# Moving the split of the cross values' weights onto GpSimd, with the context ahead of its folds

## The reference, cut to what matters

```python
ln_out = _ln(hidden_states, ln_w, ln_b)
q  = _fp8_linear_pertensor(ln_out, wq, wq_scale, q_in_scale)    # likewise k, v, qx
kvx = jnp.einsum('bsi,oi->bso', cond, w_kv_x)
kx, vx = jnp.split(kvx, 2, axis=-1)
...
xout = _gqa(qx, kx, vx).reshape(b, s, nh * d)
cat = jnp.concatenate([core, xout], axis=-1)
catq = _div_clamp_fp8(cat, proj_smooth)
return jnp.einsum('bsi,oi->bso', catq, wproj) * (proj_in_scale * proj_w_scale)
```

## Time and profile before

| | |
|---|---|
| median of 3 runs | 463.3 us (461.24 to 463.32) |
| profiled execution, its time | 463.74 us |
| profiled execution, its span | 461.9 us |
| mean granted clock of PE | 0.962 |
| busy: PE, DVE, ACT, POOL | 89%, 79%, 64%, 61% of the span |

### The profile page before, as it was taken

How to read it: one execution, slowest core, us unless ns; L and a number is a source line. 1 busy time by engine, 2 the same in 40 slices (tenths; PEclk the granted TensorE clock), 3 DMA queues, 4 the chain that set the end, 5 groups by cost and what they waited for, 6 DMA issues and landing times.

```text
span 461.9 us, 10277 instructions
## 1 busy us (share of the span) xinstructions
PE 412.3 (89%) x3127; PEld 318.3 (69%) x3127; DVE 363.6 (79%) x824; ACT 295.0 (64%) x622; POOL 282.1 (61%) x409
## 2 busy tenths in 40 slices
PE   0677899999999999999999999999899596999980
PEld 0444577777777777777777777776689385999960
DVE  5867879999998899999999989999984872333257
ACT  3587977677767767777776776776862122566620
POOL 2079676775885677677688568754550671377750
PEclk9999999999999999999999999999996688999995
DMA  8940919999900000000000000000193123344308
GB/s 208 268 184 2 171 15 325 264 321 275 272 17 0 0 0 0 0 0 0 0 0 0 0 0 0 0 1 1 41 431 146 57 104 92 115 123 138 110 5 269
DMA packets 34812, 45.68 MB, mean 99 GB/s; under 512 B 3034, under 2 KB 32223, under 8 KB 33888
## 3 DMA queue, kind: packets, MB, share of 16 engines
q1 hardware_dynamic: 26656, 35.61, 25.2%
q0 software_dynamic: 6992, 9.46, 9.3%
q10 hardware_dynamic: 1136, 0.27, 0.3%
HBM read 28.34 MB, written 24.32 MB: 114 GB/s over the span
## 4 chain that ended last, share of the span: by engine, by line
PE 76%; DVE 8%; DMA 5%; ACT 3%; POOL 3%; issue 3%; SPq 1%; POOLq 0%; ACTq 0%
PE proj_ps L938 16%; PE score_ps L965 12%; PE proj_ps L930 8%; PE pv_ps L987 7%; PE out_ps L997 7%; PE headT_ps L956 5%; PE proj_ps L1103 4%; PE headT_ps L1103 4%; PE probT_ps L973 3%; PE score_ps L956 2%; DMA cenf<-in_cen 2%; PE pv_ps L1118 2%; PE score_ps L1118 1%; DMA wp_sb<-ybuf 1%; DVE arena L1290 1%
## 5 line engine op out<-in xcount | busy, mean ns | idle before, releaser
L938 PE MATMUL proj_ps<-arena 128*128 128x512 f16 x384 | 99.4, 382 | 3.0 <-DVE arena L1333 3.0
L1341 DVE BATCH_NORM_STATS2 st<-rot 128x6 f32<-128x256 f32 x192 | 72.8, 420 | 14.5 <-ACT rot L689 13.4
L689 ACT ACTIVATE rot<-proj_ps 128x512 f32<-128x512 f32 x96 | 56.4, 587 | 22.3 <-PE proj_ps L938 20.6
L551 POOL TENSOR_TENSOR rot<-rot,cw 128x512 f32<-128x512 f32 x64 | 67.3, 1072 | 2.5
L965 PE MATMUL score_ps<-kT,qT 128*128 128x64 f32 x512 | 63.8, 279 | 0.6 <-ACT qT L724 0.5
L965 PEld LDWEIGHTS score_ps<-kT,qT 128*128 128x128 f32 x512 | 61.3, 196 | 3.0 <-ACT qT L724 2.2
L710 ACT ACTIVATE rot<-rot,cw 128x128 f32<-128x128 f32 x128 | 40.9, 390 | 30.7 <-POOL cw L545 30.7
L557 POOL TENSOR_TENSOR reg<-reg,rinv 128x512 f32<-128x512 f32 x32 | 33.4, 1043 | 42.4 <-DVE rinv L1361 42.4
L938 PEld LDWEIGHTS proj_ps<-arena 128*128 (+1 forms) x384 | 37.7, 103 | 27.3 <-issue 3.8
L930 PE MATMUL proj_ps<-arena 128*128 128x512 f16 x192 | 46.7, 379 | 0.6 <-POOL arena L507 0.6
L619 POOL DMA_INDIRECT ybuf<-arena,bslot x32 | 31.4, 982 | 19.9 <-issue 13.4
(11 more groups left out here) (219 smaller groups left out, 872.4 us busy)
## 6 DMA issues: line engine op xcount, KB each, us to landing
zbuf<-fill SPq DMA_DIRECT2D x1, 16576.5 KB, 61.5
arena<-in_wffn SPq DMA_DIRECT2D x4, 1536.0 KB, 13.8
arena<-zbuf SPq DMA_DIRECT2D x32, 128.5 KB, 2.1
wkv_stage<-in_wkvN SPq DMA_DIRECT2D x1, 2048.0 KB, 15.4
wp_sb<-in_wpT POOLq DMA_DIRECT2D x1, 2048.0 KB, 15.5
wp_sb<-ybuf SPq DMA_DIRECT2D x8, 256.0 KB, 4.5
xs<-in_x SPq DMA_DIRECT2D x2, 512.0 KB, 5.5
vv<-in_wqN POOLq DMA_DIRECT2D x1, 1024.0 KB, 12.5
```

The source lines that it names most:

```text
L551: gp.tensor_tensor(r, r, cw[:, 4 * i:4 * i + 4].unsqueeze(2).to_broadcast([P, 4, D]), ALU.mult)\
L689: act.activation(raw[c % 2][i], proj_ps[i % 2][:, :], ACT.Copy).then_inc(proj_evac, 1)
L938: mm = pe.matmul(ps, lhs, w[kind][:, ch, 512 * b:512 * b + 512], start=(k == 0), stop=(k == 3))
L1341: ins = ve.bn_stats(st[:, 4 * i + h:4 * i + h + 2, :].rearrange("p h s -> p (h s)"), raw[c % 2][i][:, h * D:(h + 2) * D].rearrange("p (h d ...
```

## The change

POOL alone now makes the four vx folds, in a new function `cross_values`: a multiply by the scale in place, a cast and a subtraction, two folds at the end of its step 1 and two at the end of its step 2. ACT and DVE skip them. The context halves move from POOL's step 0 to the head of its queue, before its four other folds. The issue of the output weights' load moves from the end of step 0 to the end of step 1, behind two of the new folds. The waits on `fold_hi` count without the vx folds, and PE's kx1 folds no longer wait for the vx folds ahead of them in the list. The new semaphore is `vx_full`.

```diff
 BY_POOL = [5, 7, 9, 11]
+VX = [j for j, (kind, b, c) in enumerate(FOLDS) if kind == "vx"]
...
         def low_on(engine, j):
 
-            return len([i for i in range(j + 1) if (i in BY_POOL) == (engine == "pool")])
+            return len([i for i in range(j + 1) if (i in BY_POOL + VX) == (engine == "pool")])
...
-            for i, j in enumerate(BY_POOL):
-                _, _, (high, low) = fold_source(j)
-                gp.wait_ge(fold_hi, j + 1)
-                gp.tensor_copy(high, fold_full[i % 2]).then_inc(fold_cast, 1)
-                gp.wait_ge(fold_cast, i + 1)
-                gp.tensor_tensor(low, fold_full[i % 2], high, ALU.subtract).then_inc(fold_pool, 1)
-
-            gp.wait_ge(prep_done, 1)
-
             def context_halves():
 
                 gp.wait_ge(ld_ctx, 16)
...
+
+            context_halves()
+            for i, j in enumerate(BY_POOL):
+                _, _, (high, low) = fold_source(j)
+                gp.wait_ge(fold_hi, ON_PE[j + 1])
+                gp.tensor_copy(high, fold_full[i % 2]).then_inc(fold_cast, 1)
+                gp.wait_ge(fold_cast, i + 1)
+                gp.tensor_tensor(low, fold_full[i % 2], high, ALU.subtract).then_inc(fold_pool, 1)
+
+            gp.wait_ge(prep_done, 1)
+
+            def cross_values(i):
+
+                j = VX[i]
+                src, scale, (high, low) = fold_source(j)
+                gp.wait_ge(ld_wkv, 16)
+                gp.tensor_scalar(src, src, scale, None, ALU.mult).then_inc(vx_full, 1)
+                gp.wait_ge(vx_full, i + 1)
+                gp.tensor_copy(high, src).then_inc(fold_cast, 1)
+                gp.wait_ge(fold_cast, len(BY_POOL) + i + 1)
+                gp.tensor_tensor(low, src, high, ALU.subtract).then_inc(fold_pool, 1)
...
-                if isinstance(n, int) and n == 0:
-                    context_halves()
                 if c == 0 and live(n, -NU):
                     inputs_over_scale(t + 1)
                 if c == 2 and live(n, -NU):
                     inputs_grid(t + 1)
-                if isinstance(n, int) and n == 0:
+                if isinstance(n, int) and n in (1, 2):
+                    cross_values(2 * n - 2)
+                    cross_values(2 * n - 1)
+                if isinstance(n, int) and n == 1:
                     load_output_weights()
...
             def fold_high(j):
 
-                if FOLDS[j][0] == "vx":
-                    act.wait_ge(ld_wkv, 16)
-                else:
-                    act.wait_ge(fold_done, ON_PE[j + 1])
+                if j in VX:
+                    return
+                act.wait_ge(fold_done, ON_PE[j + 1])
...
                 before = None if j < 2 or j in (4, 5) else j - 4 if 6 <= j < 10 else j - 2
+                if before in VX:
+                    before -= 2
                 if before in BY_POOL:
-                    pe.wait_ge(fold_hi, before + 1)
+                    pe.wait_ge(fold_hi, ON_PE[before + 1])
...
             def fold_low(j):
 
-                if j in BY_POOL:
+                if j in BY_POOL or j in VX:
                     return
-                ve.wait_ge(fold_hi, j + 1)
+                ve.wait_ge(fold_hi, ON_PE[j + 1])
```

More of the change, by code:

```diff
@@ L324, in build @@
         fold_pool = sem("fold_pool")
+        vx_full = sem("vx_full")
         ld_w = {k: sem("ld_w" + k) for k in ("k", "q", "v", "qx")}
```

## The result

The changed kernel takes 479.4 us (median of 6 runs, 478.02 to 488.18), the kernel before, now with 6 runs, 460.5. The ratio is 1.0414 with a 95% interval of 1.0347 to 1.0481: clearly slower. Executions in which the chip was in a slower state are left out of the ratios. The profiled execution took 480.54 us with a span of 478.7, each 16.8 us more than before. I forecast 475.6 us, 471.4 to 479.6; the direction and the places came out as told, the loss was larger.

The account below looks back on a forecast made before the run. The prediction took PE's start of the second tile as deciding, with POOL's queue in the prologue loaded by the change: +10.4 us to vx1 and +1.9 for the clock, 463.3 + 12.3 = 475.6 us, range 471.4 to 479.6.

Parts of the forecast that it names:

- The start of the second tile decides, and nothing is won back: Second tile's first projection on PE, before at 65.21 us: any delay there counts one to one, as regular tiles keep PE full.
- Context first: ACT's copy for fold 9 late by 4.6, most of it given back between steps 0 and 1: Head of POOL's queue: ACT's copy moves from 26.39 to 31.0 us; by POOL's end of step 1 only +1.2 remains.
- POOL ends step 1 at 51.4: POOL's coefficients and two banks of step 1, ahead of the first vx folds, end at 51.4 us, before 50.20: +1.2.
- both pauses slow the clock: Rival, chance 0.17: PE's pause at 27.4 to 31.7 also lowers the clock, another 1.9 to 4 us, giving 477.5 to 479.6.
- A vx fold costs 2.5 us, since the multiply costs what the cast costs; bounds 0.3 and 1.15: Each new POOL fold: multiply 0.70, cast 0.70, subtraction 1.10 us; two folds 5.0, the four 10.0 of the +10.4.
- The meeting with DVE: 1.0 us: POOL's second two vx folds, beside DVE's quantisation of step 0: six operations slowed, 1.0 us added, bounds 0 and 2.5.
- The load is hidden, with 3.8 us to spare: Output weights' load, issued by 58.2, lands at 71.9 us; PE's wait for it comes at 75.7.
- The floor that I gave to this rival: Rival that the load is last, chance 0.08 with cheaper folds: its landing then costs at least 6.7 us, 470.0.
- POOL's relief of DVE: DVE's first two vx subtractions, 3.04 us beside POOL's multiply, and a wait of PE's kx1 fold go away: costed at nothing.
- The idle times on POOL are used up: POOL's step 2: idle 1.17 and 3.28 us ahead of normalisation and coefficients vanish, about 0.8 staying; 3.6 us come off the sum.
- the +10.4: Start of PE's projection of vx1, at 73.5 instead of 63.04 us, once POOL's last vx fold is done.
- The clock after the pause ahead of vx1: +1.9: After PE's pause of over 6 us before vx1: 3.7 us at half speed, 1.9 us lost, lower bound 0.

Follow-up runs that it names:

- the filled kernel: The changed kernel with idle matmuls on PE in the three pauses, ahead of fold 11, vx0 and vx1: 476.5 us against 462.7 before, ratio 1.0315.
- the mended wait alone: The kernel before with only PE's kx1 folds no longer waiting for DVE's vx folds: 461.3 us against 462.7, ratio 0.9975.

## Why the prediction was right, and where it was short

The direction, the place and the wait were right. The size was short: +12.3 us forecast, +16.8 measured between the two profiled executions and +18.9 between the medians. That the median of 479.4 lies inside the range, 0.2 us under its upper end, is luck. The sum started from 463.3 us, and the six runs of the kernel before have a median of 460.5; from 463.3 either measured loss leads to 480.1 or 482.2, outside the range.

*The start of the second tile decides, and nothing is won back.* Right: +17.7 us there, +16.8 at the end of the span, and the difference is inside the scatter of that stretch.

*Context first: ACT's copy for fold 9 late by 4.6, most of it given back between steps 0 and 1.* Right in kind: the copy started 5.3 us later (31.66 against 26.39), since the context landed 0.6 later than I took from the row of before; alone this part costs 2.4 us by the medians, 3.5 by the ratio.

*POOL ends step 1 at 51.4.* It was 53.33. Of the 1.9 us, 0.6 are the later landing, and most of the other 1.3 is the clock: the first pause did slow PE (0.51 and 0.50 from 28 to 38 us). I had held this as a rival with 0.17 ("both pauses slow the clock"). It was what happened, and the filled kernel shows its price, 1.1 us there. My reason against it, that this is the shorter of the two pauses, did not carry: in the kernel with the context first alone a pause of 3.79 us was enough. Nor did the prologue of before say anything, where no pause lowered the clock: from 24 us on its longest is 1.1 us. The Trainium skill, "TensorE: Matmul & The Clock Gate", section "HAM oscillation — how this bites in real kernels", says that each such gap is paid again; the trace agrees, with three dips for three pauses.

*A vx fold costs 2.5 us, since the multiply costs what the cast costs; bounds 0.3 and 1.15.* This is the step that failed. The multiply took 1.50 us, above my upper bound, a fold 3.38. Four folds make (1.56 - 0.70) x 4 = 3.4 us, the largest part of the 5.4 by which vx1's start, 78.93, missed the forecast 73.5. I had bounded a one-input operation by the rows of other operations and taken the two-input one for a ceiling; no row showed that it was one. The Trainium skill, "GPSIMD Engine Reference", section "4.1 Engine selection", calls one-input work roughly line-rate, by which I had estimated 0.43 us; the cast's 0.61 is 1.4 times that, the multiply's 1.50 is 3.5 times. The kernels without it and with it on ACT (-7.1 and -7.7 us at the second tile) show that it was on the path.

*The meeting with DVE: 1.0 us.* It was 7.3 - 6.7 = 0.6.

*The load is hidden, with 3.8 us to spare.* Right, and with 7.2: issued at 60.07, it landed 15.6 us later at 75.7, and PE asked for it at 82.9. The floor that I gave to this rival is real: without the vx folds PE waited 0.81 us for it. That POOL's relief of DVE is worth nothing held too: the mended wait alone, 461.3 us against 462.7, can't be told from no change.

*The idle times on POOL are used up.* Right: 0.64 left of 3.28. But I took POOL's queue as the only chain there. Putting the load back gave 0.5 us, not 1.8, because ACT's roots, behind PE's projection of vx0 at the slow clock, are as late as POOL's own work. So the 1.8 us that I had counted into the +10.4 for the load's issue can't be won back by themselves: POOL's first vx fold starts 0.5 us sooner in that run already, at 52.80, and nothing more is gained behind it.

*The clock after the pause ahead of vx1: +1.9.* Measured 4.00 - 2.17 = 1.8, between the projection of vx1 and the second tile. (The prediction's last list has the second tile "near 76"; its own sum, 65.21 + 12.3, gives 77.5. Measured was 82.93.) There was a third pause, ahead of vx0, that I had costed at 0.6 us and that became 2.57, with a dip of its own.

The sum: 12.3 forecast; + 0.6 context, + 1.1 first dip, + 3.4 multiply, - 0.4 DVE, and 0.7 that I can't put to one place (among it the second dip, which shows up in the filled kernel as about 0.4) = 17.7.

## What to carry to other kernels

Before work goes to another engine, add up that engine's free time in the very stretch where it would land: here 7.4 us free, 13 to 14 added. A price for an operation that no row shows is an open bound, not one closed by the costliest row of another operation. And a pause on PE has two prices, its length and what PE does slowly after it; when a change makes PE wait at one place for as long as the pauses here that were followed by a dip (2 us and more), the second is to be in the sum, at least as a bound.

## What the runs showed of the hardware that I had not expected

POOL's multiply of 128x512 fp32 by a constant, in place, took 1.50 us (1.67 beside DVE's quantising), while its two-input multiply of the same size takes 1.04 and its cast 0.61. Whether it is the constant, the operation or the write in place was not taken apart.

Pauses of PE of 2.1, 2.57, 5.48 and 6.83 us, and in the experiments of 3.70, 3.79, 4.14 and more, were each followed by a stretch at the 1.2 GHz level, while pauses of up to 1.1 us in the prologue of before (from 24 us on), and one of 1.54 us at 24.2 in the changed kernel, were not. The length alone doesn't decide it. Late in the run of before a pause of 1.9 us was followed by a fall, and in the kernel with the load put back, between 400 and 409 us, one of 2.37 us was not. The windows (columns as in rows 2) around that one:

```profile
403.00:405.60 2.60, 0.31 (x2) 0.00 (x0) 0.81 (x2) 1.15 (x2) 0.14 (x2) 1.00 0.33 101
405.60:409.00 3.40, 2.93 (x21) 2.51 (x22) 0.00 (x0) 2.06 (x4) 0.48 (x4) 1.00 0.51 142
```

Matmuls whose results nobody reads, put into three of the pauses, kept the granted clock at 1.00 and brought the start of the second tile 3.4 us forward (3.9 less the context's earlier landing).
